# Experts of a mixture-of-experts stage: the second product with one column group per quarter of the output

## What is computed

```
C = ceil(T * K / E * CF)                        # 77 rows an expert; E = 32, K = 2, D = 512, F = 2048
xe = zeros((E, C, D)).at[flat_e, pos_d].add(x_rep, mode='drop')
he = gelu(einsum('ecd,edf->ecf', xe, w1) + b1[:, None, :], approximate=False)
ye = einsum('ecf,efd->ecd', he, w2) + b2[:, None, :]
```

## Time and profile before

| | |
|---|---|
| median of 3 runs | 2123.53 us (2120.76 to 2127.91) |
| the profiled execution | 2121.14 us, its span 2119.5 us |
| TensorE matmul busy | 1954.7 us, 92% of the span |
| TensorE weight loads busy | 1002.4 us, 47% |
| VectorE, ScalarE, GpSimd busy | 694.1, 543.6, 195.3 us |
| granted TensorE clock, mean | 0.967 of full speed |
| experts stage | about 343 to 1108 us of the span |

### The profile page before, as it was taken

How to read it: one execution, slowest core, us unless ns; L and a number is a source line. 1 busy time by engine, 2 the same in 40 slices (tenths; PEclk the granted TensorE clock), 3 DMA queues, 4 the chain that set the end, 5 groups by cost and what they waited for, 6 DMA issues and landing times.

```text
span 2119.5 us, 37580 instructions
## 1 busy us (share of the span) xinstructions
PE 1954.7 (92%) x15760; PEld 1002.4 (47%) x15760; DVE 694.1 (33%) x1499; ACT 543.6 (26%) x1115; POOL 195.3 (9%) x182
## 2 busy tenths in 40 slices
PE   5888887999999999999995999999999999999956
PEld 2444464333333333333333657575666666565633
DVE  2566651221112111221123333434343333433322
ACT  1333211222222222222111223232323333332311
POOL 1222202000000000000002000000000000000000
PEclk9999999999999999999997999999999999999977
DMA  9544137999999999999975100000000000000000
GB/s 341 206 159 159 60 149 274 396 393 378 389 375 379 358 377 373 377 360 377 374 264 198 31 21 21 26 21 27 21 17 20 27 21 21 26 14 23 11 5 5
DMA packets 86296, 374.96 MB, mean 177 GB/s; under 512 B 7782, under 2 KB 25702, under 8 KB 53432
## 3 DMA queue, kind: packets, MB, share of 16 engines
q1 hardware_dynamic: 79544, 355.71, 44.0%
q0 software_dynamic: 6656, 17.77, 2.3%
HBM read 357.73 MB, written 16.45 MB: 177 GB/s over the span
## 4 chain that ended last, share of the span: by engine, by line
PE 70%; issue 19%; POOL 4%; DVE 3%; ACT 2%; DMA 1%; SPq 1%; POOLq 0%; DVEq 0%; ACTq 0%
PE ps L1200 26%; PE ps L1378 16%; PE ps L1360 16%; POOL arena L503 4%; PE ps L1368 2%; PE ps L1572 2%; PE ps L1386 1%; DMA arena<-in_wproj0T 1%; PE ps L1502 1%; PE ps L1210 1%; ACT arena L668 1%; PE ps L1260 1%; PE ps L1349 1%; PE ps L1460 1%; PE ps L1290 1%
## 5 line engine op out<-in xcount | busy, mean ns | idle before, releaser
L1200 PE MATMUL ps<-arena 128*128 128x512 f32 (+3 forms) x3208 | 914.4, 442 | 41.8 <-ACT arena L757 14.2
L1200 PEld LDWEIGHTS ps<-arena 128*128 128x128 f32 x3208 | 549.6, 195 | 371.7 <-issue 300.2
L1378 PE MATMUL ps<-arena 128*32 128x512 f32 x3072 | 373.6, 594 | 0.0
L1360 PE MATMUL ps<-arena 128*32 128x512 f32 x3072 | 362.7, 594 | 0.6 <-issue 0.6
L503 POOL TENSOR_TENSOR arena<-arena 128x1 f32<-128x1 f32 (+3 forms) x80 | 128.2, 1602 | 1135.8 <-DVE arena L837 646.5
L1021 DVE COPY arena<-ps 128x512 f32<-128x512 f32 x96 | 66.4, 691 | 485.6 <-PE ps L1378 485.6
L1360 PEld LDWEIGHTS ps<-arena 128*32 128x32 f32 x3072 | 107.3, 109 | 226.7 <-issue 226.6
L1378 PEld LDWEIGHTS ps<-arena 128*32 128x32 f32 x3072 | 99.2, 109 | 197.6 <-issue 191.5
L718 ACT ACTIVATE arena<-ps 128x512 f32<-128x512 f32 x96 | 57.3, 597 | 354.8 <-PE ps L1360 354.8
L1112 DVE TENSOR_REDUCE arena<-ps 128x1 f32<-128x257 f32 x128 | 54.2, 423 | 162.2 <-PE ps L1460 162.2
L747 ACT ACTIVATE arena<-ps,arena 128x257 f32<-128x257 f32 x128 | 60.6, 476 | 146.3 <-PE ps L1200 145.1
(11 more groups left out here) (190 smaller groups left out, 1327.8 us busy)
## 6 DMA issues: line engine op xcount, KB each, us to landing
arena<-in_w SPq DMA_DIRECT2D x64, 4096.0 KB, 13.7
arena<-in_ctxT SPq DMA_DIRECT2D x8, 2056.0 KB, 8.5
arena<-in_ctxT SPq DMA_DIRECT2D x32, 514.0 KB, 3.8
arena<-in_ctx SPq DMA_DIRECT2D x8, 2048.0 KB
xe_rows<-arena SPq DMA_DIRECT2D x8, 616.0 KB
arena<-in_b POOLq DMA_DIRECT2D x32, 154.0 KB, 7.6
arena<-xe_rows SPq DMA_DIRECT2D x32, 154.0 KB
y_rows<-arena POOLq DMA_DIRECT2D x32, 154.0 KB, 6.1
```

The lines of the kernel that those rows point to most:

```text
L1200: ins = pe.matmul(dst, lhsT, rhs, start=(n == 0), stop=(n == len(pairs) - 1))
L1360: ins = pe.matmul(ps[q4[n], t, :], xeT[s][:, k, q4[t]], w1_sb[s][:, k, n * D:(n + 1) * D], start=(k == 0), stop=(k == KD - 1))
L1378: ins = pe.matmul(ps[q4[n], ST + t, :], hT[s][:, t, c, q4[n]], w2_sb[s][:, n * HB + c, :], start=(c == 0), stop=(c == HB - 1))
```

## The change

`result` now gives each column group one quarter of the 512 **output columns**, and lets it run through all 16 parts of the hidden dimension. So each multiplication has 128 columns instead of 512, and there are 64 instead of 16 for each `t`. The sum is complete in PSUM; `parts_out`, `folded`, `fold_sb`, `yp_sb` and their semaphores go. The result lies in one bank for each expert (`bY(s)`, 4 or 5, in turn) as four quarters on four groups of partitions, so `y_sb` and `b2_sb` get that layout, and their transfers are cut up: 8 stores and 4 loads an expert in place of 1 and 1. `hidden_out` writes `h_sb` in the order in which the transposes read it. In the last stage one small transpose goes to bank 7 in place of 5.

```diff
             def load_b2(e, s):
-                pool.dma_start(b2_sb[s][0:CAP, :],
-                               b2[bass.ts(e, 1), :].rearrange("a d -> (a d)").partition_broadcast(CAP)
-                               ).then_inc(b2_in[s], 16)
+                for q in range(HB):
+                    pool.dma_start(b2_sb[s][q4[q], :],
+                                   b2[bass.ts(e, 1), q * P:(q + 1) * P].rearrange("a d -> (a d)").partition_broadcast(T)
+                                   ).then_inc(b2_in[s], 16)
 
             def store_y(e, s, more):
                 pool.wait_ge(y_rdy, e + 1)
-                pool.dma_start(y_dram[bass.ts(e, CAP), :], y_sb[s][0:CAP, :]).then_inc(y_stored[s], 16)
+                rows_e = y_dram[bass.ts(e, CAP), :]
+                for q in range(HB):
+                    dq = slice(q * P, (q + 1) * P)
+                    pool.dma_start(rows_e[0:2 * T, dq].rearrange("(t k) d -> k t d", k=T), y_sb[s][q4[q], 0:2, :]
+                                   ).then_inc(y_stored[s], 16)
+                    pool.dma_start(rows_e[2 * T:CAP, dq], y_sb[s][q * T:q * T + (CAP - 2 * T), 2, :]
+                                   ).then_inc(y_stored[s], 16)
...
-                    act.activation(h_sb[:, t, :], ps[:, t, :], ACT.Copy).then_inc(h_out, 1)
+                    act.activation(h_sb[:, t, :].rearrange("p (c f) -> p c f", c=HB),
+                                   ps[:, t, :].rearrange("p (f c) -> p c f", c=HB), ACT.Copy).then_inc(h_out, 1)
...
-            def parts_out(e, t):
-                dve.wait_ge(y_ps, ST * e + (t + 1))
-                dve.tensor_copy(yp_sb[:, t, :], ps[:, ST + t, :]).then_inc(yp_out, 1)
-
             def result_out(e, s, i):
-                dve.wait_ge(fold_ps, e + 1)
-                dve.wait_ge(b2_in[s], 16 * i + 16)
-                wait(dve, y_stored[s], 16 * i)
-                TT(y_sb[s][0:CAP, :], ps[0:CAP, 6, :], b2_sb[s][0:CAP, :], ALU.add).then_inc(y_rdy, 1)
+                dve.wait_ge(y_ps, e + 1)
+                dve.wait_ge(b2_in[s], BD * i + BD)
+                wait(dve, y_stored[s], YD * i)
+                TT(y_sb[s], ps[:, bY(s), 0:ST * P].rearrange("p (t d) -> p t d", t=ST),
+                   bc(b2_sb[s].unsqueeze(1), P, ST, P), ALU.add).then_inc(y_rdy, 1)
...
-                        ins = pe.transpose(ps[:, t, chunk(c)], h_sb[:, t, c:D:HB], id_sb)
+                        ins = pe.transpose(ps[:, t, chunk(c)], h_sb[:, t, chunk(c)], id_sb)
...
-                wait(pe, yp_out, ST * e + (t + 1 - ST))
-                for c in range(HB):
-                    for n in range(HB):
-                        ins = pe.matmul(ps[q4[n], ST + t, :], hT[s][:, t, c, q4[n]], w2_sb[s][:, n * HB + c, :],
-                                        start=(c == 0), stop=(c == HB - 1))
-                ins.then_inc(y_ps, 1)
-
-            def folded(e):
-                pe.wait_ge(yp_out, ST * e + ST)
-                wait(pe, y_rdy, e)
-                for t in range(ST):
-                    ins = pe.matmul(ps[q4[t], 6, :], fold_sb, yp_sb[:, t, :], start=True, stop=True)
-                ins.then_inc(fold_ps, 1)
+                if t == 0:
+                    wait(pe, y_rdy, e - 1)
+                for n in range(HB):
+                    for c in range(HB):
+                        for q in range(HB):
+                            ins = pe.matmul(ps[q4[q], bY(s), chunk(t)], hT[s][:, t, c, q4[n]],
+                                            w2_sb[s][:, n * HB + c, chunk(q)],
+                                            start=(n == 0 and c == 0), stop=(n == HB - 1 and c == HB - 1))
+                if t == ST - 1:
+                    ins.then_inc(y_ps, 1)
```

More of the change, by code:

```diff
@@ L138, in perceiver_kernel @@
         xn, xnT = keep.take(D), keep.take(KD, P)
-        fold_sb = keep.take(T)
         RW = KD * F
@@ L192, in perceiver_kernel @@
         for _ in range(2):
-            b2_sb.append(W.take(D))
+            b2_sb.append(W.take(P))
             xeT.append(W.take(KD, CAPP))
-            y_sb.append(W.take(D))
+            y_sb.append(W.take(ST, P))
         rH = Region(NT * D, NT * D)
-        h_sb, yp_sb = rH.take(ST, D), rH.take(ST, D)
+        h_sb = rH.take(ST, D)
         yg = view(ring_off[1][0], 2 * NT, D)
@@ L256, in perceiver_kernel @@
             "w1_in", "w2_in", "b2_in", "xe_in", "y_stored"))
[L257 to L259 removed]
+        xeT_ps, xeT_rdy, h_ps, h_out, hT_ps, hb_rdy, hT_rdy, y_ps, y_rdy = (sem(n) for n in (
+            "xeT_ps", "xeT_rdy", "h_ps", "h_out", "hT_ps", "hb_rdy", "hT_rdy", "y_ps", "y_rdy"))
         b1_ps = sem("b1_ps")
@@ L295, in perceiver_kernel @@
         NV = 2
+        BD, YD = 16 * HB, 16 * 2 * HB
         NXT = 2 * KD + 1
@@ L408, in load_w2 @@
             def load_w2(e, s):
-                wait(sp, y_ps, ST * (e - 1))
+                wait(sp, y_ps, e - 1)
                 sp.dma_start(w2_sb[s].rearrange("p (n c) d -> p n (c d)", n=HB),
@@ L1032, in result_out @@
             def result_out(e, s, i):
-                dve.wait_ge(fold_ps, e + 1)
-                dve.wait_ge(b2_in[s], 16 * i + 16)
-                wait(dve, y_stored[s], 16 * i)
-                TT(y_sb[s][0:CAP, :], ps[0:CAP, 6, :], b2_sb[s][0:CAP, :], ALU.add).then_inc(y_rdy, 1)
+                dve.wait_ge(y_ps, e + 1)
[3 more added lines that the diff above has]
+                   bc(b2_sb[s].unsqueeze(1), P, ST, P), ALU.add).then_inc(y_rdy, 1)
             def expert(e, s, i):
                 first = isinstance(e, int) and e == 0
[L1040 to L1044, removed]
                 biased(e, s)
                 if not first:
-                    parts_out(e - 1, 2)
+                    result_out(e - 1, 1 - s, i if s == 1 else i - 1)
             for s in range(2):
@@ L1374, in result @@
                 pe.wait_ge(hT_rdy, ST * e + (t + 1))
-                wait(pe, yp_out, ST * e + (t + 1 - ST))
-                for c in range(HB):
-                    for n in range(HB):
-                        ins = pe.matmul(ps[q4[n], ST + t, :], hT[s][:, t, c, q4[n]], w2_sb[s][:, n * HB + c, :],
-                                        start=(c == 0), stop=(c == HB - 1))
-                ins.then_inc(y_ps, 1)
-            def folded(e):
-                pe.wait_ge(yp_out, ST * e + ST)
-                wait(pe, y_rdy, e)
-                for t in range(ST):
-                    ins = pe.matmul(ps[q4[t], 6, :], fold_sb, yp_sb[:, t, :], start=True, stop=True)
-                ins.then_inc(fold_ps, 1)
+                if t == 0:
[8 more added lines that the diff above has]
+                    ins.then_inc(y_ps, 1)
             def expert(e, s, i, last=False):
-                first, second = (isinstance(e, int) and e == n for n in range(2))
+                first = isinstance(e, int) and e == 0
                 ip = i if s == 1 else i - 1
                 hidden(e, s, i, 0)
-                if not (first or second):
-                    folded(e - 2)
                 hidden(e, s, i, 1)
@@ L1415, in _ @@
             expert(E - 1, 1, E // 2 - 1, True)
-            result(E - 1, 1, E // 2 - 1, 0)
-            folded(E - 2)
-            for t in range(1, ST):
+            for t in range(ST):
                 result(E - 1, 1, E // 2 - 1, t)
-            folded(E - 1)
             def head(i):
```

22 lines of the change are left out of this document (8 added, 14 removed).

## The result

The change makes the kernel slower: the median of four runs is 2281.28 us against 2123.55, a ratio of 1.074 (95% interval 1.072 to 1.076), +158 us. The prediction had the side right and the size wrong: 2171 us, with 2240 as its upper end.

The account below looks back on a forecast made before the run. TensorE's instruction stream was taken as the bound. Stream -25.7 - 8.0 + 8.6, stage end +2.5 (sum -22.6) and jumps +70 gave +47 on 2121.1, 2168.5; with 2.4 for the median 2171 us, range 2128 to 2240.

Parts of the forecast that it names:

- The stream gets shorter by -25 us: TensorE's expert-stage work without stops: fold -25.7, transposes -8.0 and product rounds +8.6 us together.
- fold: Summing partial results between experts costs TensorE 0.83 us; removing it 31 times inside the stream gives -25.7 us.
- transposes: Twelve per expert, reading without a step of 4, save 0.25 us an expert: -8.0 us, bounds -5 and -11.
- rounds: Four column-group matmuls of 128 columns take 0.110 us, 32 per row group: +8.6 us, bounds +5.6 and +21.
- End of the stage +2.5 us: After the last product, the sum, 8 store issues 0.64 us apart and landing take 7.6 us instead of 5.1.
- The turn is fetched anew, some 10 packets each: TensorE's expert-loop turn grows from 856 to 1984 records, no longer stays, and is fetched again in every turn.
- 13 jumps of 5.4 us, +70: TensorE stands at each jump back of the expert loop: 5.4 us, bounds 2.2 and 9.7; in all +29 to +126.
- the 0.5: Extra microseconds per jump for fetching beside DMA engines 95% busy; possible span 0 to 3.9 us.
- the 4.0: Microseconds of stop per jump: 4.5 us of fetch less 0.5 us of short matmuls still queued; at least 2.2.
- The clock: Slower TensorE clock after each jump's idle time: 0 to 1.8 us, half taken, 0.9 us a jump.
- The fetch cannot keep up even in line: Rival: packets late inside the new product, +70 us, plus jumps of 9.7 us (+56): about 2297 us; chance 0.07.
- its own sign of being wrong: The forecast is wrong if TensorE's idle times at jumps are under 1.7 us, or appear inside `result`.

Follow-up runs that it names:

- e3: The kernel before with only ScalarE's copy reordered, so the transposes read without a step: 2117.95 us against 2122.35, ratio 0.998.
- e4: The changed kernel, loop kept, with half of the second product left out (output differs, turn of about 1240 instructions): 2075.62 us, 0.978.
- f3: The kernel before with each 512-column multiplication in hidden and result cut into two of 256, loop kept: 2231.02 us, 1.051.
- f2: The changed kernel, loop kept, with three quarters of the expert weights not loaded from expert 2 on (output differs): 2205.04 us, 1.038.
- e1: The changed kernel with TensorE's expert loop alone written out, so no jump back is left: 2185.85 us, 1.030.
- h2: The changed kernel with TensorE's expert loop written out and three quarters of the weights from expert 2 on not loaded: 2125.52 us, 1.001.
- g1: The kernel of e3 with the new second product for odd experts only, loop kept, turn of 1449 instructions: 2116.88 us, 0.997.
- f4: The kernel before with TensorE's expert loop written out, as a control: 2125.68 us, 1.001.
- h1: The kernel of f3 (multiplications cut into halves of 256 columns) with TensorE's expert loop written out: 2130.07 us, 1.004.
- g2: The kernel of g1 with TensorE's loop written out and result put between the row groups of hidden where the new product runs: 2124.3 us, 1.001.
- e2: The changed kernel written out, with result's row groups put between those of hidden: 2160.89 us, 1.018.
- f1: The changed kernel with the mixed order of e2 but TensorE's loop kept: 2262.28 us, 1.065.

## Why the prediction was right in its side and wrong in its size

- *The stream gets shorter by -25 us* (fold, transposes, rounds): right, 22.93 measured against 23.0. In it the transposes were sized too large at -8.0: 1.65 us for twelve became 1.46, 6 us in 32 experts, and -4.4 us in the median of e3. Rounds of 0.110 us: right (e4 has 1.77 us for 16, 0.111).
- *End of the stage +2.5 us*: +1.1. The stores are issued 0.54 us apart, not 0.64, and SyncE's first issue behind them comes 6.3 us after the sum begins (1266.80 to 1273.09), not 7.6.
- *The turn is fetched anew, some 10 packets each*: right, 10. The rule of the Trainium skill that was weighed there (Runtime: NRT & Kernel Launch, Instruction fetch mechanics: 2048 instructions in TensorE's store) would let the 2007 stay; after and f3, a turn of 1655, speak against it, and the largest turn that stayed is 1449.
- *13 jumps of 5.4 us, +70*: 6.1 us, +79. The stop was 3.8 us of idle time, 4.07 from start to start, where 4.0 and 0.5 for the load of the DMA engines were predicted. With the light load of f2 it is 3.6, so the 0.5 was right and the 4.0 was too much. The clock cost 2.0 and not 0.9: half of a cost that came behind every jump was the wrong choice.
- *"The fetch cannot keep up even in line", chance 0.07*: this is the step that failed, and its own sign of being wrong (idle times inside `result`) is what the profile shows. The prediction took "at an idle 4.5 us it keeps up" and 3.5 us for a block, two ahead, and had no term for it in its sum. In the change a block of short multiplications has the pace of the fetch, 6.1 us, not that of TensorE, and the 60 stops are +98 us. The rival named its place rightly and its time (2297 against 2281) nearly; its price was put otherwise, 9.7 us for a jump and 70 for the stops, where 6.1 and 98 were measured, so that the totals agree is luck. What should have raised its chance stood in the rows read: 4.5 us for the pair of packets of the earlier trace rows in 8% of DMA load is more than the 3.5 us of a block, and in the earlier trace rows the load is 95%.

**Shown** by e1 and h2 against e1, f2, e4, f3 and g1: the loss is instruction fetch, it needs a turn that isn't resident, and in line it depends on the load of the DMA engines. (The traffic to memory fell with that load, so the two are not told apart.) Where TensorE stops in line, the load acts before the packet starts, not after. From the packet's start to the matmul behind the stop the median is 2.44 us in the kernel after (60 stops) and 2.49 in e1 (52), and under light load 2.43 in f2 (31) and 2.43 in h2 (13), all within 2.2 to 2.9. What holds a packet back before it starts is not shown. The Trainium skill (same section) has the crossing of a 16 KB border "mostly hidden"; so it is in f4 and h1, and not in e1, where the block is used in less than 6 us.

**Open**: where between 1449 and 1655 instructions a turn stops being resident; why the packet doesn't start earlier; the 4 us of the stage not assigned; and g1's end, whose way from the last product to the first scores is 42.8 us against 37.0 before. With the same cut-up stores g2 has 38.1 there, so some 4 us may be had.

## What to carry to other kernels

Before a multiplication is cut into narrower ones, count the instructions of the turn of the loop it is in (a float32 matmul is four) and look for the number of 16 KB packets a turn and the duration of the branch back: a turn that was resident and no longer is pays at each jump and, where 256 instructions last less than about 6 us beside heavy loads, at each block. If the better form is only just too long, it can be used for a part of the turn, as in g1, which at least lost nothing (2116.88 us against 2117.95 in e3). Writing the loop out takes the jumps away, but check the blocks' durations: the change written out is still at 2186 us. Spreading the short ones helped in line (e2), and with the loop kept it made the jump dearer (f1).

## What the runs showed of the hardware

- The branch back takes 0.215 us with the turn resident, 4.24 us in the change, 5.2 in f3, and 6.11 in f1, where the second of the jump's two packets begins 3.5 to 4.0 us behind the start of the branch and not 0.9 to 1.5.
- Under 0.78 to 0.88 of DMA load a stream of short instructions goes at about 6.1 us for each 256. With the load at 0.3 the stops fall from 78.4 to 21.1 us (e1, h2), while the time from a packet's start to the next matmul stays at a median of 2.4 to 2.5 us.
- The granted clock falls to 0.50 behind all 13 jumps, where TensorE stood for 3.5 to 4.2 us: ten times for about 3.4 us, three times for 6.8.
- A row group of 128 matmuls of 128 columns in four column groups takes 3.5 us with its 128 weight loads, 0.110 us for four, against 3.43 us for the 32 of 512 columns before, so the narrow column groups are nearly free on the array itself here.
